# A deformable-convolution kernel: the interpolation matrices S^T are turned by transposing DMAs on SyncE's queue, and loads of x and stores of x1 and y are issued by ScalarE

## The reference

```
x = x + attention(groupnorm(x))        # q, k, v = W x; softmax over channels of q k^T; v; W_out
x = x + deform(groupnorm(x))           # below

offset = clip(conv3x3(x), -8, 8); mask = 2 * sigmoid(conv3x3(x))
for each of 9 taps: p = bilinear sample of x at (pixel + tap + offset), times mask
y = sum over taps of w_tap @ p
out = gelu(batchnorm(y))               # statistics over all 32 images
```

## Time and profile before

| what | value |
|---|---|
| median of 3 runs | 4033.15 us (4030.4 to 4049.43) |
| the profiled execution: its own time | 4041.7 us |
| its span, first to last instruction | 4039.9 us |
| TensorE busy | 3554.5 us, 88% |
| VectorE / ScalarE / GpSimd busy | 2650.4 (66%) / 2108.1 (52%) / 1412.7 us (35%) |
| DMA | 170.89 MB, mean 42 GB/s |

### The profile page before, as it was taken

The page is one execution under the profiler, slowest core; times in us unless marked ns, Lnnn a source line. Parts: engine busy times, 40 slices in busy tenths (PEclk is TensorE's granted clock), DMA queues, the critical chain, the costliest instruction groups (busy, mean ns, idle before and its releaser), DMA issues.

```text
span 4039.9 us, 109164 instructions
## 1 busy us (share of the span) xinstructions
PE 3554.5 (88%) x38338; PEld 3036.9 (75%) x38338; DVE 2650.4 (66%) x5834; ACT 2108.1 (52%) x4790; POOL 1412.7 (35%) x1165
## 2 busy tenths in 40 slices
PE   3999999999999999999999999999999999999600
PEld 2788878888887878888887878788788888877600
DVE  3666776676777666666776676677666766776522
ACT  1555555555555555555555555555555555554422
POOL 1333333333333333434333333333333433333311
PEclk8999999999999999999999999999999999999855
DMA  2000000000000000000010000000000000000398
GB/s 63 20 11 28 28 28 20 28 28 28 10 28 28 20 28 28 28 17 21 29 28 21 28 28 28 10 28 28 28 20 28 28 24 14 28 28 10 96 370 299
DMA packets 50796, 170.89 MB, mean 42 GB/s; under 512 B 9664, under 2 KB 10880, under 8 KB 50176
## 3 DMA queue, kind: packets, MB, share of 16 engines
q1 hardware_dynamic: 39584, 136.75, 11.2%
q0 software_dynamic: 7168, 25.17, 1.6%
q10 hardware_dynamic: 3424, 0.90, 0.1%
HBM read 87.29 MB, written 75.50 MB: 40 GB/s over the span
## 4 chain that ended last, share of the span: by engine, by line
PE 65%; DVE 13%; issue 9%; DMA 4%; POOL 4%; ACT 3%; DVEq 1%; SPq 1%; ACTq 0%; POOLq 0%
PE sps L653 10%; PE acc L672 6%; PE acc L670 6%; PE acc L671 6%; PE l L581 4%; PE zps L639 3%; PE zps L643 3%; PE zps L641 3%; PE zps L640 3%; PE zps L642 3%; DVE zl L1151 3%; POOL sT L1346 3%; DMA xn<-x_scratch 2%; DVE sl L1157 2%; PE l L513 2%
## 5 line engine op out<-in xcount | busy, mean ns | idle before, releaser
L1346 POOL TENSOR_TENSOR sT<-ay,bx 128x768 f32<-128x768 f32 x768 | 1149.3, 1507 | 1394.6 <-PE sps L653 1326.2
L1157 DVE TENSOR_TENSOR sl<-sps,sh 128x384 f16<-128x384 f32 x1536 | 847.8, 552 | 560.7 <-ACT sh L896 555.9
L672 PE MATMUL acc<-zh,sl 128*128 128x192 f16 x4608 | 1134.6, 246 | 22.4 <-issue 22.4
L670 PE MATMUL acc<-zh,sh 128*128 128x192 f16 x4608 | 1134.6, 246 | 0.3 <-ACT ypm L923 0.3
L671 PE MATMUL acc<-zl,sh 128*128 128x192 f16 x4608 | 1134.5, 246 | 0.0
L896 ACT CAST sh<-sps 128x384 f16<-128x384 f32 x1536 | 741.4, 483 | 705.3 <-PE sps L653 696.9
L862 ACT CAST zh<-zps 128x288 f16<-128x288 f32 x1536 | 620.2, 404 | 668.4 <-PE zps L643 643.7
L1151 DVE TENSOR_TENSOR zl<-zps,zh 128x288 f16<-128x288 f32 x1536 | 694.2, 452 | 353.5 <-ACT zh L862 345.2
L653 PE MATMUL sps<-eye,sT 128*128 128x128 f32 x4608 | 786.3, 280 | 130.7 <-DVE sl L1157 96.6
L653 PEld LDWEIGHTS sps<-eye,sT 128*128 128x128 f32 x4608 | 531.7, 141 | 287.0 <-DVE sl L1157 158.0
L672 PEld LDWEIGHTS acc<-zh,sl 128*128 128x128 f16 x4608 | 451.3, 98 | 25.4 <-issue 25.3
(11 more groups left out here) (200 smaller groups left out, 6488.8 us busy)
## 6 DMA issues: line engine op xcount, KB each, us to landing
xin<-in_x SPq DMA_DIRECT2D x32, 512.0 KB, 5.2
xin<-in_x SPq DMA_DIRECT2D x64, 256.0 KB, 5.7
x_scratch<-x SPq DMA_DIRECT2D x32, 512.0 KB, 2.8
y_scratch<-ych SPq DMA_DIRECT2D x32, 512.0 KB, 2.7
zh<-y_scratch SPq DMA_DIRECT2D x20, 512.0 KB, 11.6
zl<-x_scratch SPq DMA_DIRECT2D x20, 512.0 KB, 12.8
out<-zh POOLq DMA_DIRECT2D x20, 512.0 KB, 9.3
x_scratch<-x SPq DMA_DIRECT2D x32, 256.0 KB, 3.5
```

What stands on the lines that cost most here:

```text
L670: pe.matmul(acc[:, 0:C], s_h, zh[:, j, ky, z], start=start and kx == 0, stop=False)
L672: mm = pe.matmul(acc[:, 0:C], s_l, zh[:, j, ky, z], start=False, stop=stop and kx == 2)
L1157: dve.tensor_tensor(one(sl), sps[u % 2][:, 0:3 * P], one(sh), ALU.subtract).then_inc(s_lo, 1)
L1346: pool.tensor_tensor(sT[:, p % ST_RING].rearrange("p k (r x) -> p k r x", r=R), a, x_, ALU.mult)\
```

## The change

S^T is split into float16 high and low parts before it is turned: ScalarE copies the 768 columns of `sT` to the high half of a slot of `sT_hl` (ring of four), VectorE subtracts to get the low half, and SyncE then issues one transposing DMA per step from `sT_hl` (128 x 1536 float16) to `s_hl` (12 blocks of 128x128). TensorE has no transposes of S left, and its products read `s_hl`. Splitting is now one operation of 768 columns per step on each engine in place of two of 384. It runs four steps ahead of the product (`S_AHEAD`), so the first four steps of an image are split in the last four units of the image before. `part0` runs six units earlier (`EARLY`). `bx` becomes a ring of two to make room in SBUF. The seven other DMAs of an image are issued by ScalarE: `convolved(b - 1)` in unit 8, `attended(b + 1)` in unit 22. The far pass, a branch for large offsets, gets its own tiles. In the diff, the first `turn_s` is SyncE's, the removed one TensorE's, `split_s` is ScalarE's, and the last lines are GpSimd's.

```diff
-        bx = sb("bx", [P, 2, TILES * TAPS, W])
+        BX_RING = 2
+        bx = sb("bx", [P, BX_RING, 2 * TAPS, W])
...
-        S_RING = 3
-        sh = sb("sh", [P, S_RING, 3, P], F16)
-        sl = sb("sl", [P, S_RING, 3, P], F16)
+        S_RING = 4
+        sT_hl = sb("sT_hl", [P, S_RING, 2, 3 * R * W], F16)
+        s_hl = sb("s_hl", [P, S_RING, 2, 3, 2, P], F16)
...
+        def prepare(part0, u, b, par, more):
+            if u + EARLY < UNITS:
+                if more:
+                    part0(u + EARLY, b + 1, 1 - par)
+            elif more == 2:
+                part0(u + EARLY - UNITS, b + 2, par)
...
+        STEPS = 3 * TILES
+        S_AHEAD = 4
+        EARLY = 6
+
+        def s_step(u):
+            if u >= UNITS - S_AHEAD:
+                return u - (UNITS - S_AHEAD), True
+            if u % 2 == 0 and u // 2 + S_AHEAD < STEPS:
+                return u // 2 + S_AHEAD, False
+            return None, False
...
+            def turn_s(p, b):
+                if p >= S_RING or not first(b):
+                    sp.wait_ge(sz_done, UNITS * b + 2 * (p - S_RING) + 2)
+                    sp.sem_inc(turn_free, 1)
+                sp.wait_ge(s_lo, STEPS * b + p + 1)
+                sp.sem_inc(turn_begun, 1)
+                slot = p % S_RING
+                sp.dma_start_transpose(s_hl[:, slot].rearrange("p h k c n -> p (h k c) n"),
+                                       sT_hl[:, slot].rearrange("p h n -> p (h n)")).then_inc(s_turned[slot], 16)
...
-            def turn_s(u, b):
-                t, ky, c = u // 6, u % 6 // 2, u % 2
-                if c == 0:
-                    pe.wait_ge(st_made, 24 * b + 3 * t + ky + 1)
-                if u >= 2 or not first(b):
-                    pe.wait_ge(s_lo, UNITS * b + u - 1)
-                g = (3 * t + ky) % ST_RING
-                for kx in range(3):
-                    mm = pe.transpose(sps[u % 2][:, kx * P:(kx + 1) * P], sT[:, g, kx, c * P:(c + 1) * P], eye32[:, :])
-                mm.then_inc(s_ps, 1)
-
             def convolve(u, b, par):
                 i, ky, c = u // 6, u % 6 // 2, u % 2
-                pe.wait_ge(s_lo, UNITS * b + u + 1)
+                if c == 0:
+                    pe.wait_ge(s_turned[u // 2 % S_RING], turned(u // 2, b))
...
-            def split_s(u, b):
-                act.wait_ge(s_ps, UNITS * b + u + 1)
-                if u >= S_RING or not first(b):
-                    act.wait_ge(sz_done, UNITS * b + u - S_RING + 1)
-                act.copy(sh[:, u % S_RING].rearrange("p k n -> p (k n)"), sps[u % 2][:, 0:3 * P]).then_inc(s_hi, 1)
+            def split_s(p, b):
+                act.wait_ge(st_made, STEPS * b + p + 1)
+                if p >= S_RING or not first(b):
+                    act.wait_ge(s_turned[p % S_RING], turned(p - S_RING, b))
+                act.copy(sT_hl[:, p % S_RING, 0], sT[:, p % ST_RING].rearrange("p k n -> p (k n)")).then_inc(s_hi, 1)
...
+                    if u == 8 and not first(b):
+                        convolved(b - 1)
+                    if u == 22 and more:
+                        attended(b + 1, more == 2)
...
                     if p >= ST_RING or not first(b):
-                        pool.wait_ge(s_ps, UNITS * b + 2 * (p - ST_RING) + 2)
+                        pool.wait_ge(s_lo, STEPS * b + p - ST_RING + 1)
```

More of the change, by code:

```diff
@@ L218, in build @@
         st_made = sem("st_made")
-        s_ps = sem("s_ps")
+        s_turned = [sem(f"s_turned{i}") for i in range(S_RING)]
+        turn_free = sem("turn_free")
+        turn_begun = sem("turn_begun")
         s_hi = sem("s_hi")
@@ L312, in pairs_of_images @@
         @contextmanager
-        def pairs_of_images(eng, start, end):
+        def pairs_of_images(eng, start, end, step=2):
             name, only = f"images_{nc.next_id()}", [eng.engine]
@@ L687, in far_pass @@
             def far_pass(b, par, more):
-                pe.wait_ge(s_lo, UNITS * (b + 1) + 2 * more)
                 pe.wait_ge(y_ch, 4 * (b + 1))
@@ L901, in part1 @@
                         split_z(g, b, par)
-                    split_s(0, b)
-                    split_s(1, b)
+                    for p in range(S_AHEAD):
+                        split_s(p, b)
+                    attended(0)
+                    prepare_second(part0)
                 for u in units:
@@ L906, in part1 @@
                         edge.append(act.mark_branch_hint_location())
-                    if u + 2 < UNITS:
-                        split_s(u + 2, b)
-                    elif more:
-                        split_s(u + 2 - UNITS, b + 1)
+                    p, of_next = s_step(u)
+                    if p is not None and not of_next:
+                        split_s(p, b)
+                    elif p is not None and more:
+                        split_s(p, b + 1)
                     if u == 24:
```

165 lines of the change are left out of this document (88 added, 77 removed).

## The result

The changed kernel takes 4332.3 us (median of 4 runs, 4321.12 to 4352.19) against 4032.94 us for the kernel before, timed beside it: ratio 1.0738, 95% interval 1.0688 to 1.0788. It is slower by 299 us; 3740 was forecast. The profiled execution took 4337.27 us.

A forecast was written before the change was run, and what follows sets the result against it. TensorE was taken to bound: 94.8 us per image plus 5.8 stretches, 2.4 waits, 2.0 issues, 1.0 first turn made 106.0, 9.4 below 115.4; times 32, with some 5 us for the first image, 3740 us. Range 3540 to 3980, own 3640 to 3890.

The forecast's parts named there:

- What bounds the kernel: Whole kernel: TensorE busy 110.59 of 115.44 us per image; four stretches with another engine full or close decide what arrives.
- TensorE's 15.8 us: TensorE, per image: 48 units lose transposes of 0.33 us each, so work falls from 110.6 to 94.8 us.
- ScalarE's and VectorE's splits: Splits before the turn: 0.93 us on ScalarE, 0.96 on VectorE; 17.5 us more per image if each met GpSimd, not expected.
- What of it arrives: Per image: four stretches where ScalarE or VectorE limits add 5.8 us to TensorE's 94.8, remaining waits 2.4, making 103.0.
- Moving part 0 ... I cost it at nothing: Part 0 six units earlier: shares of TensorE, VectorE, ScalarE and GpSimd move together, so no cost except in the unevenness.
- The clock: Granted clock 1.00 in all stretches; a fall below 1.00 because TensorE idles was a sign of a wrong forecast.
- ScalarE's issues: Five DMA issues from unit 22 delay z's copy and stall TensorE 2.0 us per image, ends 0 and 4.1.
- The turn: Transposing DMA: lands in 2 to 3 us, nothing lost in the flow; 1.0 us stall at an image's start.
- The turns bound, slower: Rival, 14%: SyncE's queue takes one turn at a time; at 5.2 us each an image takes 125 us, 4340 in all.
- The two queues hinder each other: Rival, 20%: ScalarE's issues slow down beside turns, seven costing 9.1 us per image; 111 us per image, 3890 in all.
- It does nothing: Rival, 2%: if GpSimd's S^T came late, the turn would only move a wait; GpSimd is busy 42.64 of 115.44 us.
- TensorE alone bounds: Rival, 12%: rings of four and the six-unit move even out the stretches; all 15.8 us arrive, 3532 us.

The follow-up runs named there:

- the filler: Three unused transposes of a constant per unit put back on TensorE in units 2 to 43, branch announcements moved, against the splits spread: 4123.78 us.
- the version with all three edits: Changed kernel with GpSimd's part 0 two steps later, column hats in units 0, 11, 23, and plain DMAs issued by SyncE: 4104.09 us.
- the splits spread: The version with all three edits, with the next image's first four S^T splits in units 41, 43, 45, 47 in place of 44 to 47: 4073.37 us.
- with the hats: Changed kernel with GpSimd's part 0 two steps later and ScalarE's column hats in units 0, 11, 23 in place of 3, 13, 25: 4165.47 us.
- z in four banks: The version with all three edits, with z in a ring of four PSUM banks in place of two: 4149.49 us.
- filler in five units: The splits spread, with unused transposes on TensorE only in units 15, 22, 32, 46, 47: 4002.64 us; with the loop's branch announced in unit 12, 4001.54.

## Why the prediction was wrong

- **What bounds the kernel** (right, but read too strongly). TensorE was full in most stretches. The forecast took that for the path. A bare unit now lasts 1.36 us in place of 1.68, and the filler shows that over most of the image what is taken off TensorE comes back as waiting for the other engines' chains, or as clock.
- **TensorE's 15.8 us**: right, 16.0.
- **ScalarE's and VectorE's splits**: ScalarE 0.93 forecast, 0.834 measured. VectorE 0.96 forecast, 0.958 as the median, but 1.146 as the mean:

```profile
L1194 DVE TENSOR_TENSOR sT_hl<-sT,sT_hl x768: 937/958/2239, 120.1 to 4091.8; 128x768 f16<-128x768 f32 x192
L928 ACT CAST sT_hl<-sT x768: 816/834/866, 119.2 to 4090.9; 128x768 f16<-128x768 f32 x192
```

  24 x 0.19 = 4.5 us per image go to meeting GpSimd, where I had argued from the order that they take turns. That argument failed: the mean stays at 1.099 us in the version with all three edits, where S^T is no longer late, and falls to 1.012 with the splits spread, so splits that crowd together meet GpSimd too. GpSimd pays as well: its S^T took 1.621 us on average, against 1.507 before. The Trainium skill's exclusion ("SBUF — State Buffer", Who interferes with whom) agrees with the maximum of 2.24 us; the 17.5 us of a meeting every time was too much.
- **What of it arrives: the step that failed.** The forecast kept 2.4 us of waits, added 5.8 for four stretches, 2.0 for the issues and 1.0 for the first turn, 11.2 in all. Idle time was 20.6, though the first turn cost nothing of it (in images 6 to 26 it had landed 2.4 us or more before its product). The comparison of busy times per stretch was made for stretches as the kernel before has them, and only asks whether an engine is full. The new waits are mostly chains: TensorE to ScalarE to VectorE and back, where no engine is full (the stretch at 2056). A chain's length does not shrink with TensorE's work, and what the transposes covered came out as a gap.
- **"Moving part 0 ... I cost it at nothing"**: wrong in two ways. GpSimd's list moves differently from the others', since S^T is now wanted four steps ahead, with part 0's items still in front of it (167 us with the hats). I had dismissed this rival ("If GpSimd's S^T came late") by its busy time of 42.64 us of 115.44; it was late by its place, not for want of time. And the place of part 0 moves the time by 188 and 207 us for two and eight units; no run leaves it where it was.
- **The clock** had no term: 9.5 us per image. The text named it as what would make it wrong ("if the clock falls below 1.00 in it because TensorE idles"), and the chance was worth a price. 11.2 to 20.6 and 0 to 9.5 together are 18.9 of the 19.1 us between 106.0 and 125.1.
- **ScalarE's issues**: mechanism right. 2.0 us per image forecast, 2.8 measured on the kernel before (90 us / 32) and 1.4 on the changed one (45 us / 32). The seven issues beside turns were named as a rival at 9.1 us; three loads take 1.15 us each in place of 0.53, some 1.9 us.
- **The turn**: landing 2 to 3 us forecast, 3.8 measured, and nothing waits for it; the rows of the turn itself:

```profile
L463 SPq DMA_TRANSPOSE s_hl<-sT_hl x768: 1413/1435/5610, 121.1 to 4092.8; - x192
...
DMA to landing us min/median/max: 3.6/3.8/14.7
```

  "Nothing lost in the flow" holds for the dependence and not for the queues: 110 us. The figure of 1309 ns per 128x128 block in the Trainium skill ("VectorE: DVE Perf Modes", The three transpose paths) does not scale in series: twelve blocks land in 3.8 us here.
- **The rivals.** "The turns bound, slower" gave 4340, 8 us from the result, by a mechanism that is not there: the queue is issued in 1.43 us per turn and TensorE has no wait for `s_turned`; that the number was near is luck. "The two queues hinder each other" is real, at a part of the size. "It does nothing" held the main cause of the first half, at 2%. "TensorE alone bounds", given 12%, is refuted by the result, and the filler says why.

What stays open: the 4.7 us of idle time that are left over the kernel before even with filler (9.9 against 5.2); how the 110 us of the turns divide; why the work column is 2.2 us lower with z in four banks; and the branch.

## What to carry to other kernels

- When the busiest engine is relieved, ask first what its removed work had covered. Take the chains through the other engines, with their lengths, and set them against the new, shorter unit; busy shares per stretch see full engines only.
- Putting the removed work back as an unused copy, or a part of it, is the cheapest test of this: 13.9 us put back cost 1.6.
- A move "for all engines alike" has to be read in each engine's list, the slow side engine's above all, and DMA issues belong on a queue whose engine nobody waits for. Deeper buffers may only gather small waits into large ones.

## What the runs showed of the hardware

- The granted clock follows idle time, and not simply: behind 2.78 us of waiting TensorE stood at the 1.2 GHz level from 1998.9 to 2002.3, and in the spread version, behind 0.86 us at unit 22 half-clock time came to 1.7 us per image, but behind 1.90 us at unit 38 of the same version there was none. What the engine did in the units ahead differs; which of it decides was not settled.
- The loss can be larger than the wait: z in four banks had 0.4 us more idle time per image and 2.8 us more loss to the clock. Work with no use, placed in the waits, was worth 71 us.
- The issue of a load of x on ScalarE's queue took 1.15 us (median) beside SyncE's turns and 0.52 without them, and the load landed in 7.6 us in place of 6.0. The stores of x1 issued just before showed no such thing: 0.35 and 0.52 us with turns and without.
- TensorE's branch at the end of an image took 0.4 to 0.6 us on average in most versions and 3.5 to 3.7 in two that differ from these only in filler; the loop's branch took 0.35 us, and 3.5 and 3.1 in the two versions with filler in five units.
